# Layer 1 of a four-layer graph stack: element-wise work moved to ScalarE, order and placing of the channel steps changed

## What is computed

```python
h = jnp.maximum(_layernorm(x, axis=-1), 0.0)
feat = jax.nn.softplus(h * (INV_SQRT2 * w0[0, 0]) + b0[0])
scores = feat * wa + ba
mask = adj > 0
logits = where(mask, scores[:, None], -1e9)
attn = jax.nn.softmax(logits, axis=2)
out = jnp.einsum('bijd,bjd->bid', attn, feat)
x = x + out
```

## Time and profile before

| | us |
|---|---|
| median of three runs (2087.2 to 2091.23) | 2087.61 |
| profiled execution | 2091.14 |
| its span in the trace | 2089.3 |
| busy: TensorE, VectorE, ScalarE, GpSimd | 1925.6, 1723.7, 1160.1, 1075.9 |
| mean granted TensorE clock | 0.972 |

### The profile page before, as it was taken

The page is one execution under the profiler, slowest core; times in us unless marked ns, Lnnn a source line. Parts: engine busy times, 40 slices in busy tenths (PEclk is TensorE's granted clock), DMA queues, the critical chain, the costliest instruction groups (busy, mean ns, idle before and its releaser), DMA issues.

```text
span 2089.3 us, 94507 instructions
## 1 busy us (share of the span) xinstructions
PE 1925.6 (92%) x43528; PEld 1576.5 (75%) x43528; DVE 1723.7 (83%) x2084; ACT 1160.1 (56%) x1404; POOL 1075.9 (51%) x776
## 2 busy tenths in 40 slices
PE   4988669899999999999999999999999999966998
PEld 2777669887777777777777777777777777745887
DVE  4999869977788888888888888888878888845998
ACT  3444333334666666666666666666666666632342
POOL 4787588852235535354444544555544544335653
PEclk8999879999999999999999999999999999977999
DMA  6000000001111111111111111111111111100111
GB/s 173 4 3 4 3 2 2 2 2 33 33 34 33 35 33 30 37 33 34 36 32 37 33 33 33 33 33 33 33 33 33 33 33 33 33 12 8 24 29 34
DMA packets 88251, 61.20 MB, mean 29 GB/s; under 512 B 45616, under 2 KB 86832, under 8 KB 87856
## 3 DMA queue, kind: packets, MB, share of 16 engines
q1 hardware_dynamic: 85632, 54.57, 11.4%
q10 hardware_dynamic: 2224, 0.59, 0.1%
HBM read 8.98 MB, written 4.19 MB: 6 GB/s over the span
## 4 chain that ended last, share of the span: by engine, by line
PE 68%; DVE 16%; POOL 8%; issue 3%; ACT 3%; DMA 1%; SPq 1%; ACTq 1%; DVEq 0%; POOLq 0%
PE ACC L1292 30%; PE S L1410 22%; DVE ring L1130 5%; DVE ring L999 4%; PE AX L1453 3%; PE S L1389 3%; PE AX L1462 2%; PE AX L1430 2%; POOL sp_log L641 1%; POOL ln_sq L644 1%; PE S L1340 1%; PE AX L1272 1%; PE AX L1282 1%; ACT ring L839 1%; DVE ch_rden L1115 1%
## 5 line engine op out<-in xcount | busy, mean ns | idle before, releaser
L1292 PEld LDWEIGHTS ACC<-V,ring 128*64 128x64 f32 x28672 | 961.1, 139 | 193.4 <-DVE ring L999 67.5
L1130 DVE TENSOR_TENSOR ring<-ring,mask_self_t 128x1024 f32<-128x1024 f32 x640 | 894.4, 1407 | 192.6 <-ACT ring L839 188.4
L1292 PE MATMUL ACC<-V,ring 128*64 128x65 f32 x28672 | 984.7, 223 | 38.3 <-DVE ring L999 34.8
L839 ACT ACTIVATE ring<-S,dot_bias 128x1024 f32<-128x1024 f32 x640 | 713.8, 1116 | 416.0 <-PE S L1410 379.5
L1410 PE MATMUL S<-FA 128*64 128x512 f16 x5120 | 667.2, 383 | 8.8 <-DMA FA<-lo 8.7
L1410 PEld LDWEIGHTS S<-FA 128*64 128x64 f16 x5120 | 254.5, 110 | 169.3 <-ACT ring L839 16.2
L999 DVE SCALAR_TENSOR_TENSOR ring<-S,pair_q,mask_t 128x1024 f32<-128x1024 f32 x256 | 314.5, 1272 | 12.0 <-DVE f_max L1011 4.1
L657 POOL TENSOR_TENSOR EV_both<-score,recip 128x512 f32<-128x512 f32 x64 | 124.3, 1943 | 314.5 <-DVE score L1137 314.5
L1389 PE MATMUL S<-parts,mask_t 128*128 128x128 bf16 x3072 | 181.2, 224 | 29.6 <-DVE X L1119 18.3
L1389 PEld LDWEIGHTS S<-parts,mask_t 128*128 128x128 bf16 x3072 | 179.6, 100 | 31.1 <-issue 28.8
L725 ACT ACTIVATE accs<-ACC 128x520 f32<-128x520 f32 x112 | 67.0, 599 | 173.0 <-PE ACC L1292 173.0
(11 more groups left out here) (118 smaller groups left out, 1970.5 us busy)
## 6 DMA issues: line engine op xcount, KB each, us to landing
FA<-hi SPq DMA_DIRECT2D x320, 64.0 KB, 2.0
FA<-lo SPq DMA_DIRECT2D x320, 64.0 KB, 2.0
X<-in_x SPq DMA_DIRECT2D x16, 256.0 KB, 5.1
ring<-in_adj SPq DMA_DIRECT2D x8, 512.0 KB, 9.5
out_x<-X SPq DMA_DIRECT2D x16, 256.0 KB, 2.6
wh<-in_wh_t ACTq DMA_DIRECT2D x2, 64.0 KB, 7.1
bh_bc<-in_bh ACTq DMA_DIRECT2D x1, 128.0 KB, 10.0
w_gat<-in_w_gat ACTq DMA_DIRECT2D x4, 16.0 KB, 3.7
```

The source lines that it names most:

```text
L839: act.activation(ring[:, jt, :], S[jt % 2][:, :], ACT.Exp, bias=dot_bias[:, n % 2:n % 2 + 1])\
L1130: dve.tensor_tensor(ring[:, jt, :], ring[:, jt, :], mask_self_t[:, jt, :], ALU.mult)\
L1292: last = pe.matmul(acc_of(t)[rows, :], ring[:, jt, t * P + c * CUT:t * P + (c + 1) * CUT], values, start=(jt == 0 and t % 4 == 0), stop=(j ...
```

## The change

ScalarE takes over from VectorE zt (now only the ReLU of the norm, without the factor w0), with w0 now applied as the scale of the two operations behind it: az (|w0 z + b0|) and relu_z. It also takes the square of the centered values of layer 1 from GpSimd (layer 2's stays). ScalarE waits for feat of the batch before ahead of writing relu_z, and VectorE's EV_rest names its wait for the third part of the batch before. In its step GpSimd makes the score first and `ln_scale` behind it. Steps -5, -4 and -3 go into unit 14 (VectorE: behind tiles 1, 4 and 7), steps -2 and -1 into unit 15 (behind tiles 2 and 5). On GpSimd the first two steps of a unit stand between `gat_divide` and `gat_add`, the third behind `gat_add`; on ScalarE all stand behind `gat_below`.

```diff
--- before.py
+++ after.py
@@ -400,7 +400,11 @@
                 return cur + EARLY if cur + EARLY < B else None
             return {1: B - 2, 3: B - 1}.get(cur)
 
-        STEPS_BESIDE = {1: -5, 2: -4, 4: -3, 5: -2, 7: -1}
+        STEPS_BESIDE = {(B - 2, 1): -5, (B - 2, 4): -4, (B - 2, 7): -3, (B - 1, 2): -2, (B - 1, 5): -1}
+
+        def steps_beside(cur):
+
+            return [STEPS_BESIDE[cur, jt] for jt in range(T) if (cur, jt) in STEPS_BESIDE]
 
         def channel_layer(step, first_norm, first_unit):
 
@@ -508,8 +512,9 @@
                     pool.wait_ge(y_made, 2 * B)
                 pool.wait_ge(ln_dve, 4 * n + 2)
                 pool.tensor_tensor(tiles(ln_xc[:, :]), x_of(b), cols(ln_mean[:, :]), ALU.subtract).then_inc(ln_pool, 1)
-                pool.wait_ge(ln_pool, 4 * n + 1)
-                pool.tensor_tensor(ln_sq[:, :], ln_xc[:, :], ln_xc[:, :], ALU.mult).then_inc(ln_pool, 1)
+                if layer == 2:
+                    pool.wait_ge(ln_pool, 4 * n + 1)
+                    pool.tensor_tensor(ln_sq[:, :], ln_xc[:, :], ln_xc[:, :], ALU.mult).then_inc(ln_pool, 1)
 
             def ln_scale(layer, b):
 
@@ -593,24 +598,19 @@
                         gat_norm(layer, cur + 3)
                     if late is not None:
                         stat_rstd(layer, late)
-                    if cur > 0 and (layer == 3 or cur < B - 1):
+                    steps = steps_beside(cur) if layer == 0 else []
+                    for k in steps[:2]:
+                        channel_step(k, k % 2)
+                    if cur > 0:
                         gat_add(layer, cur - 1)
+                    for k in steps[2:]:
+                        channel_step(k, k % 2)
                     if layer == 0 and 2 <= cur < 2 + T:
                         add_diagonal(cur - 2)
-                if layer == 0:
-                    for jt in sorted(STEPS_BESIDE):
-                        channel_step(STEPS_BESIDE[jt], STEPS_BESIDE[jt] % 2)
-                    gat_add(layer, B - 2)
                 gat_divide(layer, B - 1)
                 gat_add(layer, B - 1)
 
             def channel_step(k, par):
-                b = k + 4
-                if exists(b):
-                    wait(pool, ch_zt, b)
-                    if b == 0:
-                        y_is_read(AX_AT["T", 0, B - 1])
-                    ln_scale(1, b)
                 b = k + 2
                 if exists(b):
                     pool.wait_ge(ch_feat, b + 1)
@@ -620,6 +620,12 @@
                     pool.wait_ge(ch_scaled, b + 1)
                     pool.tensor_tensor(tiles(score[:, :]), tiles(score[:, :]), chans(shift_bc[:, :]), ALU.add)\
                         .then_inc(ch_score, 1)
+                b = k + 4
+                if exists(b):
+                    wait(pool, ch_zt, b)
+                    if b == 0:
+                        y_is_read(AX_AT["T", 0, B - 1])
+                    ln_scale(1, b)
                 b = k + 5
                 if exists(b):
                     ln_center(1, b)
@@ -797,9 +803,8 @@
                         gat_factors(layer, cur + 1)
                     if cur > 0 and layer == 0:
                         gat_below(cur - 1)
-                if layer == 0:
-                    for jt in sorted(STEPS_BESIDE):
-                        channel_step(STEPS_BESIDE[jt], STEPS_BESIDE[jt] % 2)
+                    for k in steps_beside(cur) if layer == 0 else []:
+                        channel_step(k, k % 2)
                 gat_sums(layer, B - 1)
                 if layer == 0:
                     gat_below(B - 1)
@@ -812,8 +817,12 @@
                     act.activation(parts[:, 1 - par, 0], EV[:, :, :], ACT.Copy).then_inc(ch_p1, 1)
                 b = k + 3
                 if exists(b):
+                    act.wait_ge(ln_pool, 4 * b + 4)
+                    act.activation(zt[:, :], ln_y[:, :], ACT.Relu).then_inc(ch_zt, 1)
                     act.wait_ge(ch_zt, b + 1)
-                    act.activation(az[:, :], zt[:, :], ACT.Abs, bias=b0_c[:, :]).then_inc(ch_az, 1)
+                    act.activation(az[:, :], zt[:, :], ACT.Abs, bias=b0_c[:, :], scale=w0_c[:, :]).then_inc(ch_az, 1)
+                    wait(act, ch_feat, b)
+                    act.activation(relu_z[:, :], zt[:, :], ACT.Relu, bias=b0_c[:, :], scale=w0_c[:, :]).then_inc(ch_relu, 1)
                     act.wait_ge(ch_az, b + 1)
                     act.activation(sp_log[:, :], az[:, :], ACT.Exp, scale=-1.0).then_inc(ch_exp, 1)
                     act.wait_ge(ch_exp, b + 1)
@@ -827,6 +836,10 @@
                     act.wait_ge(ch_score, b + 1)
                     wait(act, ch_r1, b)
                     act.activation(EV[:, :, D:2 * D], tiles(score[:, :]), ACT.Exp).then_inc(ch_e, 1)
+                b = k + 5
+                if exists(b):
+                    act.wait_ge(ln_pool, 4 * b + 1)
+                    act.activation(ln_sq[:, :], ln_xc[:, :], ACT.Square).then_inc(ln_pool, 1)
 
 
             def weights(m):
@@ -1071,26 +1084,20 @@
                             node_max(layer, cur + 2)
                         if jt == 6 and cur > 0 and layer == 0:
                             gat_elu(cur - 1)
-                        if layer == 0 and cur == B - 1 and jt in STEPS_BESIDE:
-                            channel_step(STEPS_BESIDE[jt], STEPS_BESIDE[jt] % 2)
+                        if layer == 0 and (cur, jt) in STEPS_BESIDE:
+                            channel_step(STEPS_BESIDE[cur, jt], STEPS_BESIDE[cur, jt] % 2)
                 gat_reciprocal(layer, B - 1)
                 if layer == 0:
                     gat_elu(B - 1)
 
             def channel_step(k, par):
-                b = k + 3
-                if exists(b):
-                    dve.wait_ge(ln_pool, 4 * b + 4)
-                    wait(dve, ch_az, b)
-                    dve.tensor_scalar(zt[:, :], ln_y[:, :], 0.0, w0_c[:, :], ALU.max, ALU.mult).then_inc(ch_zt, 1)
-                    dve.wait_ge(ch_zt, b + 1)
-                    dve.tensor_scalar(relu_z[:, :], zt[:, :], b0_c[:, :], 0.0, ALU.add, ALU.max).then_inc(ch_relu, 1)
                 b = k + 4
                 if exists(b):
                     ln_var_of(1, b)
                 b = k + 1
                 if exists(b):
                     dve.wait_ge(ch_p1, b + 1)
+                    wait(dve, ch_p3, b)
                     dve.tensor_tensor(EV_rest[:, :, :], EV[:, :, :], parts[:, 1 - par, 0], ALU.subtract)\
                         .then_inc(ch_r1, 1)
                 b = k + 5
```

## The result

| | before | after |
|---|---|---|
| median of the runs shown (us) | 2088.11 (2087.2 to 2091.23, 4 runs) | 2071.72 (2069.47 to 2074.92, 4 runs) |
| profiled execution, its span | 2091.14, 2089.3 | 2073.83, 2072.0 |
| mean granted clock | 0.972 | 0.976 |
| TensorE's step 0, step 2, step 12 start | 274.08, 307.45, 430.81 | 269.36, 297.68, 415.50 |
| first dot products of layer 2 | 479.77 | 464.81 |

After over before is 0.992, 95% interval 0.990 to 0.994: 16.4 us faster, with 20.3 forecast. Step 2 comes 9.8 us earlier (13.0 forecast), the ten steps behind it take 117.82 instead of 123.36 (6.8 forecast, 5.5 found), and from step 12 to layer 2's first dot products after takes 49.31 where before took 48.96 (0.5 to be gained, 0.35 lost). That is 15.0 at layer 2's start, where the forecast had 20.3; what lies behind it is within the spread of single runs (2069.5 to 2074.9).

The account below looks back on a forecast made before the run. VectorE and GpSimd were taken as full in layer 1. The way in (13.0), the pitch (6.8) and a shorter low-clock start (0.5) together give 20.3 us, from the 2087.6 median to 2067.3, range 2057 to 2080.

Parts of the forecast that it names:

- What bounds: Layer 1, ten steps: VectorE (118.8 of 123.4 us) and GpSimd (104.8) are full, ScalarE two thirds empty.
- part 1: Pitch of TensorE's steps 2 to 11 in layer 1: falls from 12.34 to 11.65 us, gaining 6.8.
- VectorE's 2.18 us: Time a step that VectorE loses with zt (1.25) and relu_z (0.93) in layer 1.
- E(k-1): End of TensorE's step k-1, which releases ScalarE's first part of batch k+1; the two-step chain of 23.3 us starts there.
- D(k): End of VectorE's step k, its add of batch k-1 into X; forecast 12.3 us behind E(k-1).
- Part 2: Way into layer 1, up to TensorE's step 2: start at 294.5 instead of 307.45 us, gaining 13.0.
- The stalls: VectorE's waits for ScalarE's results in units 14 and 15 of layer 0: 1.6, 1.5 and 4.2 us.
- The tail: The three TensorE steps from step 12 on, 33.95 us before: a shorter gap gives back about 0.5.
- TensorE-bound: Rival for the steps of layer 1: ScalarE's five operations hide, pitch 10.95, gain 27.3, total 2060 us; chance 0.13.
- The chain takes it all: Rival for the steps of layer 1: pitch stays 12.3, gain 13.0 + 0.5, total 2074 us; chance 0.11.
- The way in fails: Rival: spread steps stall the weights as now, step 2 at 307, only 7.3 us gained, total 2080; chance 0.04.
- The slower clock: Rival: TensorE's first layer-1 steps stay at the lower clock, 9.2 us each; three such give 2095; chance 0.03.

Follow-up runs that it names:

- e5: The kernel after with both ReLUs (zt, relu_z) back on VectorE, placing, GpSimd's order and the square as in after: 2067.1 us, 0.9899 of before.
- e12: The kernel before with the new placing of the steps and the square on ScalarE, power still first, ReLUs on VectorE: 2069.8 us, 0.9908 of before.
- e11: The kernel before with the new placing of the steps and the score first on GpSimd, ReLUs on VectorE, square on GpSimd: 2076.5 us, 0.9944 of before.
- e4: The kernel after with the square of layer 1 back on GpSimd: 2076.7 us, 0.9943 of before.
- e8: The kernel after with ScalarE's second part ahead of relu_z, Exp and Ln, and VectorE's feat behind the add into X: 2060.8 us, 0.9862 of before.
- e6: The kernel after with two more 128x512 ReLUs, output unread, behind Ln in ScalarE's queue: 2075.9 us, 0.994 of before.
- e1: The kernel after with steps -5 to -1 all in unit 15 again, as before: 2077.9 us, 0.9947 of before.

## Why the prediction was right or wrong

**What bounds.** Right that VectorE and GpSimd filled the steps, and right that the loop of before ran over GpSimd's whole step, for whose EV the first part waited 22.4 us. But the prediction didn't ask which of its edits opens that loop: part 1 starts from VectorE's 2.18 us.

**Part 1, the new pitch.** The steady number is right: E(k-1) to D(k) 12.28 against 12.3, two steps 23.31 against 23.3. The terms were off in ways that cancel: feat (0.98) stands in the chain where the sum had the second part (1.06), which runs beside it; the third part took 2.06 for 1.63, X 0.70 for 1.0, and ScalarE's five operations 3.26 (335.12 to 338.38) for 3.4. So the price of the queue that the ReLU move makes was right, with some luck in its terms. The mean over the ten steps, 11.78, is not 11.65: the sum had no term for the low clock at the start of step 2, which the earlier trace rows shows (0.50), and the first pair took 25.41, 2.1 more than a steady one, of which the shorter last pair (22.47) gave 0.8 back.

**Part 1, the step that failed.** "VectorE loses zt and relu_z: 1.25 + 0.93 = 2.18 us a step" as the source of the gain. e5 and e12 show that GpSimd's loss of the square is the source (12.34 to 11.61 by it alone) and that the ReLU move takes 0.24 a step back. Only with the square left on GpSimd does the ReLU move bring pitch, and then 0.23 (e11 to e4). Nor was there a fixed 2.18 to lose: relu_z, 0.93 on the mean before, is a mix of 0.49 and 1.38 there, and takes 0.49 in e5 and e12 with the same operands; with the square gone VectorE holds 11.46 with both. What hid this, and makes the near hit on the pitch partly luck: a forecast built from the new loop needs no account of the old one, so it came out right with the credit on the wrong edit. Had each edit been priced alone ahead of the sum, the square would have stood as the relief of GpSimd, for which the first part waits, and the ReLUs as a relief that brings the chain with it.

**Part 2, the way in.** Right until the end of layer 0: the sums of unit 15 end and step 0 starts at 269.36 (269.0), VectorE's step 0 at 273.41 (272.9) and ends at 279.97 (279.2). The stalls were 1.47, 0.62 and 3.35 for 1.6, 1.5 and 4.2, TensorE's wait for the copy-out 4.97 for 4.7. The mis-sized term is steps 0 and 1. GpSimd and VectorE in order of time in after:
```profile
274.80 2.33 POOL L618 TENSOR_TENSOR score<-feat,wa_bc 128x512 f32<-128x512 f32 x1
277.22 1.67 POOL L621 TENSOR_TENSOR score<-score,shift_bc 128x512 f32<-128x512 f32 x1
278.85 2.62 POOL L523 TENSOR_TENSOR ln_rstd<-ln_ve,neg_half 128x8 f32<-128x8 f32 x1
```
```profile
284.42 0.69 DVE L1001 TENSOR_REDUCE ln_var<-ln_sq 128x8 f32<-128x512 f32 x1 [4.45 <-ACT ln_sq L842]
...
290.28 2.00 DVE L1115 TENSOR_TENSOR parts<-EV_both,parts 128x1024 bf16<-128x1024 f32 x1 [0.26 <-ACT parts L833]
```
I had priced GpSimd's operations at 1.3 and 1.65, as they run alone; beside VectorE they took 2.33, 1.67 and 2.62. So the square of batch 5 was ready at 284.4, not 282.1, and ScalarE's first part of batch 2, which waits for GpSimd's EV, started only at 284.99, where the prediction had EV at 282.9:
```profile
284.99 1.06 ACT L817 ACTIVATE parts<-EV_both 128x1024 bf16<-128x1024 f32 x1 [0.60 <-POOL EV_both L635]
```
The third part and X behind it took 2.00 and 1.22, and step 2 came at 297.68 instead of 294.5. Of these 3.2 us 2.1 are GpSimd's; of the rest 0.7 is a slip of the sum, for 282.9 and the chain of 12.3 give 295.2, not 294.5. The rows for stretched durations stood in the earlier trace rows (score 1.71 and 1.36, power 2.46, third part 1.63); they belonged here too, for in steps 0 and 1 both engines work as they do in steps 2 to 11, and would have covered about half of GpSimd's lateness. The Trainium skill's page SBUF — State Buffer (Who interferes with whom) says that VectorE's operations with two SBUF inputs contend with GpSimd's reads; these lengths agree with it, as does X beside an idle and a working GpSimd (0.70 in after, 1.23 in e4), though no run took all of GpSimd's work away to show the cause by itself.

**The tail.** The 0.5 for a shorter low-clock start came and more: steps 12 to 14 took 32.67 (415.50 to 448.17) for before's 33.95. Step 15, behind gaps of 0.82 and 1.51, ran 12.51 instead of 10.88 and took 1.6 back. At layer 2's start the forecast was thus 5.3 us too good: 3.2 for the way in, 1.3 for the pitch, 0.8 for the tail. The medians differ by more than the traces up to there, 16.4 against 15.0, so that the total misses by 3.9 only.

**The rivals.** TensorE-bound didn't come; once the chain was cut it did, at 10.86 for the 10.95 of the rival. That e8's total (2060.8) is also its 2060 is chance in part: e8's way in was 11.4 us shorter than before's where the rival had 13.0. The chain takes it all: no, 11.66 steady. The way in fails: no. The slower clock: no, TensorE's steps 0 and 1 took 22.56 together, 0.78 more than the 21.78 of steps 4 and 5.

## What to carry to other kernels

Before crediting a gain to an engine's relief, look who ends the wait of the loop: two engines can look full in the busy times while only one of them closes the loop. Work moved to an idle engine costs its place in that engine's queue, not its duration; ask what stands between two operations that belong to one hand-over, and put the hand-over first. Where two engines lengthen each other's operations, price both loaded everywhere, at the ends of the pipeline too, and don't take a mean duration for work that would be saved.

## What the runs showed of the hardware that was not expected

An operation of ScalarE of 128x512 took 0.61 to 0.63 us with constants (the same Exp 0.614 in after, 0.631 in before), 0.707 to 0.723 with a bias from a tile, 0.80 to 0.81 with bias and scale from tiles.

VectorE's tensor_scalar of 128x512 has two durations, by what GpSimd does when it starts. Between 300 and 412 us, in the six kernels that have them on VectorE, zt took 0.47 to 0.48 us each time GpSimd was idle at its start and 1.26 to 1.50 each time it was at work, relu_z 0.48 to 0.49 and 1.37 to 1.38, with the same operands. The means of the earlier trace rows, 1.25 and 0.93, are mixes of the two.

TensorE's step 15 took 12.51, 12.51 and 12.45 in after, e6 and e1, and 10.88 in before and the other ten, behind the same two gaps of 0.82 and 1.50 or 1.51. Over its first 3 us the granted clock was 0.53 in after and 1.00 in e12. What decides it stays open.
